# A two-layer graph network kernel: the first root operation behind picks and a spread, ranks ahead of the seeds, two homes for the rows of the last tile, and the power ahead of the gathers

## The reference

```
# layer 0
adj0    = adj + I
dis     = adj0.sum(2) ** -0.5
x1      = layernorm(x + (dis * adj0 * dis) @ (x @ W) + bias)
# layer 1, h = x1
m_j, m_i = h @ W1[:D], h @ W1[D:]
msg[i,j] = gelu(layernorm(m_j[j] + m_i[i] + b1) * g1 + be1)     # exact gelu
agg[i]   = sum_j msg[i,j] * adj[i,j]
upd      = layernorm(concat(h, agg) @ W2 + b2) * g2 + be2
out      = layernorm(h + upd)
```

## Time and profile before

| | |
|---|---|
| median of 3 runs | 3537.92 us (3535.61 to 3540.91) |
| the profiled execution | 3535.7 us, span 3533.7 us |
| mean granted TensorE clock | 0.973 |
| PE, PEld busy | 3198.2 us (91%), 2943.3 us (83%) |
| ACT busy | 3042.6 us (86%) |
| DVE busy | 3008.2 us (85%) |
| POOL busy | 2104.7 us (60%) |
| DMA | mean 101 GB/s |

### The profile page before, as it was taken

How to read it: one execution, slowest core, us unless ns; L and a number is a source line. 1 busy time by engine, 2 the same in 40 slices (tenths; PEclk the granted TensorE clock), 3 DMA queues, 4 the chain that set the end, 5 groups by cost and what they waited for, 6 DMA issues and landing times.

```text
span 3533.7 us, 87356 instructions
## 1 busy us (share of the span) xinstructions
PE 3198.2 (91%) x26504; PEld 2943.3 (83%) x26505; DVE 3008.2 (85%) x6816; ACT 3042.6 (86%) x8038; POOL 2104.7 (60%) x2628
## 2 busy tenths in 40 slices
PE   4899999999989998999998999989999999999988
PEld 2788888888878888888887888888888888888887
DVE  3689988889978898888898888988888988888987
ACT  3788889898968988888987989888889898989887
POOL 3556665556645566655566555666555666555652
PEclk7999999999989999999999999999999999999999
DMA  2333333233332333323332323333323333323231
GB/s 73 106 98 106 104 115 106 88 107 106 101 102 83 110 106 97 123 94 96 111 107 94 109 87 106 107 97 122 102 89 111 106 98 121 108 82 111 91 96 45
DMA packets 284214, 355.29 MB, mean 101 GB/s; under 512 B 28208, under 2 KB 242736, under 8 KB 283696
## 3 DMA queue, kind: packets, MB, share of 16 engines
q1 hardware_dynamic: 250928, 231.55, 22.5%
q0 software_dynamic: 32768, 117.47, 8.8%
HBM read 223.09 MB, written 125.83 MB: 99 GB/s over the span
## 4 chain that ended last, share of the span: by engine, by line
PE 50%; DVE 22%; issue 10%; ACT 10%; POOL 6%; DMA 1%; DVEq 1%; ACTq 0%; SPq 0%; POOLq 0%; PEldq 0%
PE agg_even_ps L1323 9%; PE z_even_ps L1364 8%; PE z_odd_ps L1364 8%; PE agg_odd_ps L1323 6%; DVE pick L1078 6%; DVE spread L1107 4%; POOL table L514 3%; DVE msg L1053 2%; PE z_even_ps L1360 2%; PE z_odd_ps L1360 2%; ACT tmp L713 2%; ACT root L658 2%; PE p_ps L1175 2%; PE p_ps L1244 2%; PE agg_odd_ps L1244 2%
## 5 line engine op out<-in xcount | busy, mean ns | idle before, releaser
L713 ACT ACTIVATE tmp<-nbr,r_sb 128x128 f32<-128x128 f32 x4032 | 1262.5, 389 | 24.9
L1078 DVE SCALAR_TENSOR_TENSOR pick<-rank,root_p 128x512 f32<-128x512 bf16 (+3 forms) x1536 | 914.8, 625 | 98.3 <-PE z_odd_ps L1364 53.2
L514 POOL DMA_INDIRECT table<-stage,row_id x512 | 747.0, 1459 | 155.8 <-issue 145.1
L1107 DVE SCALAR_TENSOR_TENSOR spread<-nbr 128x512 f32<-128x512 bf16 (+3 forms) x1536 | 814.8, 557 | 6.5 <-PE agg_even_ps L1323 5.5
L698 ACT ACTIVATE msg<-msg 128x768 f32<-128x768 f32 x768 | 646.7, 842 | 16.0 <-issue 8.3
L529 POOL COPY root_extra<-root_p 128x32 f32<-128x32 f32 (+4 forms) x768 | 315.7, 411 | 518.7 <-ACT root_p L672 514.7
L1364 PEld LDWEIGHTS z_odd_ps<-mi_g,pick 128*128 128x128 f32 x4608 | 587.1, 198 | 26.0 <-issue 0.5
L1323 PE MATMUL agg_odd_ps<-spread,msg 128*128 128x128 f32 x4608 | 597.5, 281 | 4.5 <-issue 3.6
L1364 PE MATMUL z_odd_ps<-mi_g,pick 128*128 128x129 f32 x4608 | 600.6, 282 | 0.0
L1364 PEld LDWEIGHTS z_even_ps<-mi_g,pick 128*128 128x128 f32 x4608 | 567.1, 192 | 25.6 <-issue 0.2
L1364 PE MATMUL z_even_ps<-mi_g,pick 128*128 128x129 f32 x4608 | 579.0, 275 | 0.0
(11 more groups left out here) (219 smaller groups left out, 4609.4 us busy)
## 6 DMA issues: line engine op xcount, KB each, us to landing
nbr<-table SPq DMA_DIRECT2D x128, 640.0 KB, 5.0
adj_g<-in_adj SPq DMA_DIRECT2D x32, 1024.0 KB, 5.9
nbr_root<-table SPq DMA_DIRECT2D x128, 256.0 KB, 5.4
nbr_extra<-table SPq DMA_DIRECT2D x384, 70.0 KB
nbr_extra<-table SPq DMA_DIRECT2D x128, 90.0 KB
nbr_extra<-table SPq DMA_DIRECT2D x256, 40.0 KB
x_g<-in_x SPq DMA_DIRECT2D x32, 256.0 KB, 3.1
table<-stage,row_id POOLq DMA_INDIRECT x512, 4.6
```

Of the source, the lines that this page charges most:

```text
L514: pool.indirect_dma_start(table[q], bass.IndirectOffsetOnAxis(ap=row_id[:, jt * TB + it:jt * TB + it + 1], axis=0), stage[:, jt, it, :], N ...
L713: last = act.activation(tmp[:, c % 2, n - FROM[u], :], half_row, ACT.Identity, scale=r_sb[:, c % 2, n - FROM[u]:n - FROM[u] + 1])
L1078: ins = dve.scalar_tensor_tensor(into.rearrange("p k n -> p (k n)"), rank[:, it % 2, span], float(MARK + t), root_p[:, it % 2, span], ALU. ...
L1107: ins = dve.scalar_tensor_tensor(into, ranks(nbr[:, it, jt:jt + count, A_RANK:A_ROOT]), float(MARK + t), nbr[:, it, jt:jt + count, A_ADJ:A ...
```

## The change

- `half` is gone. Square, product and second square of a tile are now kept in the place of the finished root in the rows (`halfway`); `own` of layer 0 uses `sqi` instead. The first square of a tile therefore waits for the scatters of the graph before.
- `stage` becomes `rows_sb`, and tile 3 has a second home, `last_rows`, for graphs with q = 1. Writers of tile 3 wait for the scatters of the graph before the last one.
- VectorE's first root operation (tile 0, s = 18) moves from place 0 to place 3, behind the picks and one spread.
- ScalarE runs `sort` ahead of `prepare` in step s = 17: the rank copy comes ahead of `mj_g` and the root.
- GpSimd runs `sort` ahead of `prepare`, and the gathers of tile 3 are made two steps later (s = 4): behind the power, ahead of bias sum and edges.

```diff
-T_RANK, T_ROOT, T_EXTRA = 3, 4, (6, 6, 5, 6)
+T_RANK, T_ROOT, T_EXTRA = 3, 4, (6, 6, 5, 8)
...
-        half = sb("half", [P, TB, N])
...
-        stage = sb("stage", [P, TB, TB, ROW])
+        rows_sb = sb("rows_sb", [P, TB, TB, ROW])
+        last_rows = sb("last_rows", [P, TB, ROW])
...
+        def stage(q, jt):
+
+            return last_rows[:, :, :] if jt == TB - 1 and q else rows_sb[:, jt, :, :]
+
+        def halfway(q, jt):
+
+            return stage(q, jt)[:, :, A_ROOT:ROW]
...
+        def written(jt, a):
+
+            return max(a - 1, 0) if jt == TB - 1 and isinstance(a, int) else a - 1 if jt == TB - 1 else a
...
-                    own = half[:, 0, :].rearrange("p (t o) -> p t o", t=TB)
+                    own = sqi[:, :].rearrange("p (t o) -> p t o", t=TB)
...
-                        wait_alone(pool, p_mask, a * TB)
+                        wait_alone(pool, p_fill, a * NF - (NF - F_MIT - 1))
...
-                if a is not None:
-                    prepare(a, (i + AHEAD) // GC % 2 ^ 1, s)
                 k, t = cx.sorted(i)
                 if k is not None:
                     sort(cx.tiles + k, k, t)
                 if a is not None:
+                    prepare(a, (i + AHEAD) // GC % 2 ^ 1, s)
                     scatter(a, (i + AHEAD) // GC % 2 ^ 1, s)
...
-                        if not is_int(a, 1):
+                        if not is_int(a, 2 if jt == TB - 1 else 1):
                             for it in range(TB):
-                                act.wait_ge(p_scat[jt][it], a * 16)
-                        act.copy(stage[:, jt, :, A_ADJ:A_MJ], p.rearrange("p (i n) -> p i n", i=TB)).then_inc(p_ev, 1)
+                                act.wait_ge(p_scat[jt][it], written(jt, a) * 16)
+                        act.copy(stage(q, jt)[:, :, A_ADJ:A_MJ], p.rearrange("p (i n) -> p i n", i=TB)).then_inc(p_ev, 1)
...
-                        act.activation(half[:, jt, :], root[:, jt, :], ACT.Square).then_inc(p_sq, 1)
+                        if not is_int(a, 2 if jt == TB - 1 else 1):
+                            for it in range(TB):
+                                act.wait_ge(p_scat[jt][it], written(jt, a) * 16)
+                        act.activation(halfway(q, jt), blocks(root[:, jt, :]), ACT.Square).then_inc(p_sq, 1)
...
+                k, t = cx.sorted(i)
+                if k is not None and s == S_SEED:
+                    sort(cx.tiles + k, k, t)
                 if a is not None:
                     prepare(a, (i + AHEAD) // GC % 2 ^ 1, s)
-                k, t = cx.sorted(i)
-                if k is not None:
+                if k is not None and s != S_SEED:
                     sort(cx.tiles + k, k, t)
...
-                    if (s, slot) == (S_ROOT + jt, 0):
+                    if (s, slot) == (S_ROOT + jt, 3 if jt == 0 else 0):
                         dve.wait_ge(p_sq, a * TB + (jt + 1))
-                        dve.scalar_tensor_tensor(half[:, jt, :], v, EPS, half[:, jt, :], ALU.add, ALU.mult).then_inc(p_new, 1)
+                        dve.scalar_tensor_tensor(halfway(q, jt), blocks(v), EPS, halfway(q, jt), ALU.add, ALU.mult).then_inc(p_new, 1)
```

More of the change, by code:

```diff
@@ L265, in adj_resnorm_kernel, with blocks @@
         XL = len(LOADS) * 16
+        def stage(q, jt):
+            return last_rows[:, :, :] if jt == TB - 1 and q else rows_sb[:, jt, :, :]
+        def halfway(q, jt):
+            return stage(q, jt)[:, :, A_ROOT:ROW]
+        def blocks(row):
+            return row.rearrange("p (i n) -> p i n", i=TB)
+        def written(jt, a):
+            return max(a - 1, 0) if jt == TB - 1 and isinstance(a, int) else a - 1 if jt == TB - 1 else a
         def ranks(rows):
@@ L483, in prepare @@
                     for jt in range(TB):
-                        if not is_int(a, 1):
+                        if not is_int(a, 2 if jt == TB - 1 else 1):
                             for it in range(TB):
-                                wait_alone(pool, p_scat[jt][it], a * 16)
-                        last = pool.tensor_copy(stage[:, jt, :, A_MJ:A_RANK], mj_g[:, jt, :].unsqueeze(1).to_broadcast([P, TB, D]))
+                                wait_alone(pool, p_scat[jt][it], written(jt, a) * 16)
+                        last = pool.tensor_copy(stage(q, jt)[:, :, A_MJ:A_RANK], mj_g[:, jt, :].unsqueeze(1).to_broadcast([P, TB, D]))
                     last.then_inc(p_copy, 1)
@@ L514, in scatter @@
                     pool.indirect_dma_start(table[q], bass.IndirectOffsetOnAxis(ap=row_id[:, jt * TB + it:jt * TB + it + 1], axis=0),
-                                            stage[:, jt, it, :], None).then_inc(p_scat[jt][it], 16)
+                                            stage(q, jt)[:, it, :], None).then_inc(p_scat[jt][it], 16)
             def sort(n, k, t):
@@ L604, in prepare @@
                         act.wait_ge(r_fill, a * TB + (jt + 1))
-                        act.copy(ranks(stage[:, jt, :, A_RANK:A_ROOT]), t_ps[:, 0, :].rearrange("p (i n) -> p i n", i=TB)).then_inc(r_ev, 1)
+                        act.copy(ranks(stage(q, jt)[:, :, A_RANK:A_ROOT]), t_ps[:, 0, :].rearrange("p (i n) -> p i n", i=TB)).then_inc(r_ev, 1)
                 if s == S_SUP:
@@ L662, in prepare @@
                             act.wait_ge(p_seed, a + 1)
-                        act.activation(half[:, jt, :], root[:, jt, :], ACT.Square).then_inc(p_sq, 1)
+                        if not is_int(a, 2 if jt == TB - 1 else 1):
+                            for it in range(TB):
+                                act.wait_ge(p_scat[jt][it], written(jt, a) * 16)
+                        act.activation(halfway(q, jt), blocks(root[:, jt, :]), ACT.Square).then_inc(p_sq, 1)
                     if s == S_ROOT + jt:
                         act.wait_ge(p_new, a * TB + (jt + 1))
-                        act.activation(half[:, jt, :], half[:, jt, :], ACT.Square, bias=cube_col[:, :], scale=CUBE_K).then_inc(p_cube, 1)
+                        act.activation(halfway(q, jt), halfway(q, jt), ACT.Square, bias=cube_col[:, :], scale=CUBE_K).then_inc(p_cube, 1)
             def sort(n, k, t):
@@ L936, in prepare @@
                     v, y = var[:, jt, :], root[:, jt, :]
[L937 removed]
+                    if (s, slot) == (S_ROOT + jt, 3 if jt == 0 else 0):
                         dve.wait_ge(p_sq, a * TB + (jt + 1))
[L939 removed]
+                        dve.scalar_tensor_tensor(halfway(q, jt), blocks(v), EPS, halfway(q, jt), ALU.add, ALU.mult).then_inc(p_new, 1)
                     if (s, slot) == (S_ROOT + jt + 1, 0):
                         dve.wait_ge(p_cube, a * TB + (jt + 1))
[L942 to L943 removed]
+                        dve.scalar_tensor_tensor(halfway(q, jt), halfway(q, jt), CUBE_REST, blocks(y), ALU.add, ALU.mult).then_inc(p_mask, 1)
             def finish(e, s, slot):
@@ L1174, in prepare @@
                         for mt in range(TB):
-                            last = mm(dst, stage[:, mt, it, A_ADJ:A_MJ], sup[:, mt, :], start=(mt == 0), stop=(mt == TB - 1))
+                            last = mm(dst, stage(q, mt)[:, it, A_ADJ:A_MJ], sup[:, mt, :], start=(mt == 0), stop=(mt == TB - 1))
                     if s == S_PROD + 1:
```

3 lines of the change are left out of this document (removed).

## The result

The changed kernel takes 3450.97 us (median of 4 runs, 3449.77 to 3452.04), beside 3539.41 us for the kernel before in the same series (4 runs, 3535.61 to 3546.71): ratio 0.9748, 95% interval 0.9731 to 0.9765, 88 us less. The forecast was 3528 us, with a range down to 3505: right in sign, far too small.

A forecast was written before the change was run, and what follows sets the result against it. ScalarE was taken to bound the root stretch, not VectorE. 27 ordinary graphs by (+0.4 - 0.5) = -3, three odd ones -5, the first -2: -10 in all, 3525.7, or 3528 beside the median; range 3505 to 3547.

The forecast's parts named there:

- the 4.02 us: VectorE's idle time before its first root operation (line 939), claimed off the path because ScalarE bounds the root stretch.
- rival 2: Root stretch: VectorE's idle time is on the path after all, 1.5 us gained per graph, 47 us, 3491; chance 0.05.
- Term a: Root stretch: ScalarE's pause goes, small delays are added, line 1051 starts 0.15 us earlier; bounds 0 and 0.3.
- Term b: Root stretch: one 3.3 us TensorE stop brings the low clock, 0.3 to 1.0 us later; +0.4 per ordinary graph.
- Term c: With the power ahead of the gathers, one pick escapes blocking and `dis` comes 0.5 us earlier; bounds 0 and 1.2.
- part A: Root stretch, 782 to 807, where picks and a spread fill VectorE's idle time; net +0.4 us per ordinary graph.
- part B: Stretch around `dis`, 826 to 842: power ahead of gathers and two homes; 0.5 us gained per ordinary graph.
- Odd graphs: Three graphs where VectorE waits for the power gain 1.6 us each, 5 us; the first graph gains 2 us.
- no wait of ScalarE at the fourth copy: Sign that the forecast is right: no idle time of ScalarE at its fourth copy.
- ScalarE's 0.33 us pause: Root stretch: ScalarE idles 0.33 us before 794.37, for VectorE; its absence was a sign that the forecast is right.
- The single TensorE stop of 3 us: Sign that the forecast is right: one stop over 3 us before the second z, a granted clock of 0.5 behind it.
- rival 4: At z_even behind a 3.3 us stop, the clock costs 1.7 us, 1.0 comes through, `dis` gains nothing: 3558; chance 0.17.

## Why the prediction was wrong, point by point

- **"VectorE is early for one step, and then waits for the same `tmp`: the 4.02 us are not on the path, ScalarE is."** This is the step that failed. Line 1051 at 797.60 is `msg<-z_even`. Its `tmp` belongs to the `r_sb` of z_even, which ScalarE made at 793.05, and the one of 796.42 belongs to z_odd and the next step:

```profile
792.87 0.15 ACT L709 COPY r_sb<-z_even_ps 128x6 f32<-128x6 f32 x1
793.05 0.99 ACT L713 ACTIVATE tmp<-nbr,r_sb 128x128 f32<-128x128 f32 x3
...
796.25 0.14 ACT L709 COPY r_sb<-z_odd_ps 128x6 f32<-128x6 f32 x1
796.42 0.99 ACT L713 ACTIVATE tmp<-nbr,r_sb 128x128 f32<-128x128 f32 x3
```

  The 0.19 us that I read as a wait was chance, and the 0.05 us in my sum for line 1051 stands on no row. The row of 797.60 itself told it: it has no idle time before it, so VectorE was waiting for nothing. It had been at work since line 939. The root operation alone took 1.33 us out of this stretch. That is rival 2, priced at 1.5 us per graph and given a chance of 0.05. Its price was right for this stretch, but its 3491 us was still 40 us too high: the rest of the 88 us comes from the power's move, and from what each of the two adds to the other.
- **Term a, ScalarE 0.15 us earlier by the shift.** Its cost side was right: the early rank copy makes interval 1 0.24 us longer, and taking it out gave 5 us.
- **Term b, the low clock, 0.4 us later.** The sign was wrong. TensorE does not make one stop of 3.3 us but stops of 1.68 and 1.91. Behind the first graph there were 26 stretches at 1.2 GHz that began within 20 us behind a root before, 6 after, 3 with the root operation alone and 24 with the power alone. So the root operation's place did that too. What the low clock would have cost behind a 3.3 us stop stays open, since that stop never came. The Trainium skill (TensorE: Matmul & The Clock Gate, on HAM oscillation), which I set against the change, says that the matmuls behind an idle gap start cold once the gap is long enough. The one stop of 9.90 us shown in the last section agrees. Behind the 1.91 us of idle time here they run at full pace, and in 25 of 31 graphs no 1.2 GHz stretch began near root; but in the kernel before no stop longer than 2.08 us stood ahead of its 26, so the length of one stop does not tell the two kernels apart.
- **Term c, `dis` 0.5 us earlier, not over 0.9.** The mechanism was right, blocked picks; the size was not. Intervals 12 and 13 lose 2.28 us. I counted only the pair right ahead of `dis`; the pair before it is blocked as well as soon as VectorE comes early, which the change makes it do. The cap failed because TensorE's 0.69 us is its room at today's times: its own work ahead of that comes earlier too. The cap had some truth, since 1.65 us is given back in 14 to 16, and 0.83 comes in 17.
- **Parts taken one by one.** I added part A and part B. The runs show that each raises the worth of the other: the blocked picks eat what part A gains in its stretch, and the power's move is worth 31 us alone and 58 for a VectorE that is early.
- **Odd graphs.** The three that waited 1.67 us for the power fell from 107.0 or 107.1 us to 103.2 or 103.3; that is 3.8 us each, 1.1 more than the 2.7 by which the median period fell, where I gave them 1.6. In the first graph the 12.41 us wait is 10.12 now, but the period there fell only from 84.1 to 83.5 us, so the 2 us forecast did not come.
- **What to look for.** VectorE's wait before line 959 (3.27, forecast near 3), no wait of ScalarE at the fourth copy, and picks ahead of `dis` under 2.56 us came, and ScalarE's 0.33 us pause is gone. The single TensorE stop of 3 us did not come, nor the 1 us wait for `tmp` in the step after (0.15). The sign that I named for rival 2, a period over 1 us shorter, did.
- **A slip in rival 4.** It takes TensorE's loss to count only beyond 0.7 us. Half of its price of 1.7 us would then let 0.15 us through, not 0.5, which gives about 3535 us and not 3545; the upper end of the range, 3547, leans on that figure.

## What to carry to other kernels

Before a wait is declared off the path, check at its next meeting point that the late engine really waits there, and that names and buffers of producer and consumer belong to the same step; a row without idle time before it waits for nothing. The worth of a wait is not its length: 2.05 us of VectorE for the own sum was worth nothing, and a move that looked like 0.5 us was worth 1.9. Parts that speed up the same engine in turn should be priced together, at the times that the first part brings about.
